# One decoder layer on one core: attention steps regrouped by head half, and the next scores moved between the halves of the transposes

## The reference

```python
scores = jnp.einsum('bhqd,bhkd->bhqk', q, k) * inv_sqrt_d
scores = jnp.maximum(scores + attention_mask, jnp.finfo(scores.dtype).min)
w = jax.nn.softmax(scores, axis=-1)
attn_output = jnp.einsum('bhqk,bhkd->bhqd', w, v)
a_scores = jnp.einsum('bhqd,bhkd->bhqk', q, a_k) * inv_sqrt_d
a_scores = jnp.tanh(gate) * jax.nn.softmax(a_scores, axis=-1)
attn_output = attn_output + jnp.einsum('bhqk,bhkd->bhqd', a_scores, a_v)
return attn_output @ Wo
```

## Time and profile before

| | us |
|---|---|
| median of 3 runs | 3539.64 (3532.39 to 3540.34) |
| the profiled execution | 3538.9 |
| its span in the trace | 3537.1 |
| TensorE busy in the span | 3087.3 |
| VectorE busy | 1727.0 |
| ScalarE busy | 1349.5 |
| mean granted TensorE clock | 0.96 |

### The profile page before, as it was taken

How to read it: one execution, slowest core, us unless ns; L and a number is a source line. 1 busy time by engine, 2 the same in 40 slices (tenths; PEclk the granted TensorE clock), 3 DMA queues, 4 the chain that set the end, 5 groups by cost and what they waited for, 6 DMA issues and landing times. The chain is left out here.

```text
span 3537.1 us, 98301 instructions
## 1 busy us (share of the span) xinstructions
PE 3087.3 (87%) x43074; PEld 1955.8 (55%) x43074; DVE 1727.0 (49%) x4747; ACT 1349.5 (38%) x3283; POOL 475.1 (13%) x591
## 2 busy tenths in 40 slices
PE   4899999999999999999984999999999999825786
PEld 3566656565655655565552666565565655512453
DVE  1545454455544454454444355555555555644613
ACT  0333333333333333333331355555555555611210
POOL 0211211112111111211110211011110111000000
PEclk9999999999999999999996999999999999967987
DMA  3010010100101001010001000000000000020311
GB/s 131 26 38 11 26 38 17 38 11 26 39 17 38 11 26 38 17 35 14 26 3 61 10 7 4 10 1 10 10 1 10 1 10 1 2 107 24 143 48 48
DMA packets 90921, 100.63 MB, mean 28 GB/s; under 512 B 38144, under 2 KB 84480, under 8 KB 89088
## 3 DMA queue, kind: packets, MB, share of 16 engines
q1 hardware_dynamic: 90496, 94.34, 8.1%
HBM read 90.00 MB, written 4.33 MB: 27 GB/s over the span
## 5 line engine op out<-in xcount | busy, mean ns | idle before, releaser
L299 PE MATMUL dr_p<-x_t,dr_w_g 128*128 128x512 f32 x1536 | 749.7, 616 | 26.8 <-DMA dr_w_g<-in_w_in 13.5
L1221 ACT ACTIVATE xa_probs<-xa_probs,xa_low 128x256 f32<-128x256 f32 x1024 | 420.9, 496 | 2.2 <-DVE xa_low L1300 2.2
L299 PEld LDWEIGHTS dr_p<-x_t,dr_w_g 128*128 128x128 f32 x1536 | 270.5, 192 | 248.4 <-issue 239.5
L1300 DVE CUSTOM_DVE_ANT_0 xa_probs<-xa_s,xa_mask 128x256 f32<-128x256 f32 x512 | 215.0, 420 | 387.8 <-PE xa_s L1134 387.8
L1146 PE MATMUL xa_t<-ident,xa_probs 128*128 128x128 f32 x2048 | 285.4, 279 | 43.7 <-ACT xa_probs_t L1228 43.7
L662 DVE SCALAR_TENSOR_TENSOR dr_acc<-dr_p,dr_taps,dr_acc 128x510 f32<-128x510 f32 (+2 forms) x384 | 285.7, 744 | 27.9 <-ACT dr_acc L556 18.9
L1228 ACT ACTIVATE xa_probs_t<-xa_t 128x512 f32<-128x512 f32 x256 | 152.8, 597 | 365.8 <-PE xa_t L1146 365.8
L1146 PEld LDWEIGHTS xa_t<-ident,xa_probs 128*128 128x128 f32 x2048 | 225.1, 142 | 109.4 <-issue 93.6
L1134 PE MATMUL xa_s<-xa_keys,xa_q_pair 32*128 32x512 f32 x1024 | 258.9, 618 | 7.7 <-DVE xa_low L1300 7.0
L696 DVE TENSOR_TENSOR dr_yx<-dr_yx,dr_g 128x512 f32<-128x512 f32 x128 | 88.1, 688 | 335.1 <-PE dr_g L363 335.1
L1310 DVE COPY xa_probs_t<-xa_t 128x512 f32<-128x512 f32 x256 | 176.3, 689 | 93.8 <-PE xa_t L1146 93.8
(11 more groups left out here) (291 smaller groups left out, 5060.6 us busy)
## 6 DMA issues: line engine op xcount, KB each, us to landing
dr_alpha<-alpha_rows SPq DMA_DIRECT2D x64, 254.0 KB, 4.2
dr_w_g<-in_w_in SPq DMA_DIRECT2D x48, 256.0 KB, 5.6
dr_alpha<-alpha_rows SPq DMA_DIRECT2D x32, 256.0 KB, 5.4
x_t<-in_x_t SPq DMA_DIRECT2D x1, 4096.0 KB, 12.1
tokens<-in_x_tok SPq DMA_DIRECT2D x1, 4096.0 KB, 21.3
dr_wo_g<-in_w_out SPq DMA_DIRECT2D x8, 512.0 KB, 3.9
xa_ctx_b<-in_ctx_t SPq DMA_DIRECT2D x8, 512.0 KB, 3.7
ff_tall<-in_fw_o SPq DMA_DIRECT2D x1, 4096.0 KB, 12.2
```

Source lines behind the costliest of these rows:

```text
L299: mm = pe.matmul(bank[:, :], w_g[:, k, m, :], x_t[:, k, 2 * S * batch:2 * S * (batch + 1)], start=(k == 0), stop=(k == KC - 1))
L1221: op = act.activation(at, at, ACT.Exp, bias=low[:, u % 3, h, j, kind:kind + 1], scale=-1.0)
L1300: op = v.tensor_tensor_reduce(out=probs[:, u % 3, h, j, kind, :], in0=bank_s[h][j][:, kind * S:(kind + 1) * S], in1=mask[:, par, q, :] if ...
```

## The change

The steps stay 128. A step v now holds one head half h of all four pairs of a tile: the four scores use the four groups of 32 partitions, where they used two of them twice. `tops`, `exps`, `scored`, `topped` and `exped` count per pair i. `weigh` runs after every step for its h, with 16 matmuls, so `probs_t` holds two steps. On PE, `score(v+1)` stands between the second and the third group of transposes of step v. Both pieces of other work stand behind the transposes: `inner` is early or else late, `outer` is late where there is an early one. On ACT `copy(u, 0)` moves ahead of the early piece. DVE's order stays.

```diff
+        def inner(u):
+            return early(u) or late(u)
+        def outer(u):
+            return late(u) if early(u) else None
...
+        def place(v):
+            g = v // 2
+            q, t = divmod(g % (QT * XT), XT)
+            return g // (QT * XT) % 2, q, t, v % 2
...
+            def turn_probs(v):
+                for i in range(4):
+                    if i == 2 and v + 1 < LAST:
+                        score(v + 1)
+                    wait(pe, exped, 4 * v + i + 1)
+                    wait(pe, copied[i % 2], 2 * v + i // 2)
...
+            def weigh(v):
+                wait(pe, copied[0], 2 * (v + 1))
+                wait(pe, copied[1], 2 * (v + 1))
...
             for u in range(LAST):
-                if u + 1 < LAST:
-                    score(u + 1)
-                if early(u):
-                    pe_make(pe, early(u))
                 turn_probs(u)
-                if late(u):
-                    pe_make(pe, late(u))
-                if u % 2:
-                    weigh(u // 2)
+                if inner(u):
+                    pe_make(pe, inner(u))
+                if outer(u):
+                    pe_make(pe, outer(u))
+                weigh(u)
...
             for u in range(LAST):
+                copy(u, 0)
                 if early(u):
                     act_take(act, early(u))
-                copy(u, 0)
                 copy(u, 1)
```

More of the change, by code:

```diff
@@ L986, in cross_phase @@
         val = a.sb("val", [P, 2, 2, KT, PAIRS, 3, XD])
[L987 to L989 removed]
+        probs = a.sb("probs", [P, 3, 4, 2, S])
+        low = a.sb("low", [P, 3, 4, 2])
+        probs_t = a.sb("probs_t", [P, 2, 4, 2, KT, P])
         mixed = a.sb("mixed", [P, 2 * 2 * P])
@@ L994, in cross_phase @@
         attn_t = a.sb("attn_t", [P, KC, P])
-        bank_s = [[a.bank(f"s{h}{j}") for j in range(2)] for h in range(2)]
+        bank_s = [a.bank(f"s{i}") for i in range(4)]
         bank_t = [a.bank(f"t{j}") for j in range(2)]
@@ L1004, in cross_phase @@
         turned_by, rotated = sem("turned_by"), sem("rotated")
-        scored = [sem(f"scored{h}") for h in range(2)]
-        topped = [sem(f"topped{h}") for h in range(2)]
-        exped = [sem(f"exped{h}") for h in range(2)]
+        scored, topped, exped = sem("scored"), sem("topped"), sem("exped")
         turned = [sem(f"turned{j}") for j in range(2)]
@@ L1125, in pe_all @@
         def pe_all(pe):
[L1126 to L1154, removed]
-                for kind in range(2):
[L1156 to L1166, removed]
+            def score(v):
+                if v % HALVES == 0:
+                    wait(pe, rotated, 4 * (v // HALVES + 1))
+                    wait_taken(pe, ("ak1", v // HALVES))
+                par, q, t, h = place(v)
+                for i in range(4):
+                    wait(pe, topped, 4 * (v - 1) + i + 1)
+                    pe.matmul(bank_s[i][:, :], q_pair[32 * i:32 * i + 32, par, t, h, q * P:(q + 1) * P],
+                              keys[32 * i:32 * i + 32, par, t].rearrange("p k n -> p (k n)"), start=True, stop=True)\
+                        .then_inc(scored, 1)
@@ new lines, in turn_probs @@
+            def turn_probs(v):
+                for i in range(4):
+                    if i == 2 and v + 1 < LAST:
+                        score(v + 1)
+                    wait(pe, exped, 4 * v + i + 1)
+                    wait(pe, copied[i % 2], 2 * v + i // 2)
+                    for kind in range(2):
+                        for kt in range(KT):
+                            at = (kind * KT + kt) * P
+                            mm = pe.transpose(bank_t[i % 2][:, at:at + P], probs[:, v % 3, i, kind, kt * P:(kt + 1) * P], ident)
+                    mm.then_inc(turned[i % 2], 1)
@@ new lines, in weigh @@
+            def weigh(v):
+                wait(pe, copied[0], 2 * (v + 1))
+                wait(pe, copied[1], 2 * (v + 1))
+                par, q, t, h = place(v)
+                if h == 0:
+                    wait(pe, mixed_taken, v // 2)
+                if v % HALVES == 0:
+                    wait_taken(pe, ("av1", v // HALVES))
+                for kind in range(2):
+                    at = (kind * 2 + h) * P
+                    for kt in range(KT):
+                        for i in range(4):
+                            mm = pe.matmul(bank_o[32 * i:32 * i + 32, at:at + P], val[:, par, kind, kt, 4 * t + i, h:h + 2],
+                                           probs_t[:, v % 2, i, kind, kt, :], start=(kt == 0), stop=(kt == KT - 1))
+                            if (kind, kt) == (1, KT - 1):
+                                mm.then_inc(weighed, 1)
@@ L1214, in act_all, with exps, copy @@
         def act_all(act):
[L1215 to L1228, removed]
+            def exps(v):
+                for i in range(4):
+                    wait(act, topped, 4 * v + i + 1)
+                    for kind in range(2):
+                        at = probs[:, v % 3, i, kind, :]
+                        op = act.activation(at, at, ACT.Exp, bias=low[:, v % 3, i, kind:kind + 1], scale=-1.0)
+                    op.then_inc(exped, 1)
+            def copy(v, m):
+                wait(act, turned[0], 2 * v + m + 1)
+                wait(act, weighed, 4 * (v - 1))
+                act.activation(probs_t[:, v % 2, 2 * m].rearrange("p k t n -> p (k t n)"), bank_t[0][:, :], ACT.Copy)\
                     .then_inc(copied[0], 1)
@@ L1246, in act_all @@
                     g = u // 2
-                    wait(act, weighed, 4 * (g + 1))
+                    wait(act, weighed, 8 * (g + 1))
                     if g:
@@ new lines, in dve_all, with tops, copy @@
+        def dve_all(dve):
+            def tops(v, m):
+                if v % HALVES == 0 and m == 0:
+                    wait(dve, mask_guarded, v // HALVES + 1)
+                wait(dve, turned[0], 2 * (v - 2))
+                wait(dve, turned[1], 2 * (v - 2))
+                par, q, t, h = place(v)
+                for i in (2 * m, 2 * m + 1):
+                    wait(dve, scored, 4 * v + i + 1)
+                    for kind in range(2):
+                        op = dve.tensor_tensor_reduce(out=probs[:, v % 3, i, kind, :], in0=bank_s[i][:, kind * S:(kind + 1) * S],
+                                                      in1=mask[:, par, q, :] if kind == 0 else zeros[:, :], scale=-1.0,
+                                                      scalar=-LOWEST_F32, op0=ALU.add, op1=ALU.min,
+                                                      accum_out=low[:, v % 3, i, kind:kind + 1])
+                    op.then_inc(topped, 1)
+            def copy(v, m):
+                wait(dve, turned[1], 2 * v + m + 1)
+                wait(dve, weighed, 4 * (v - 1))
+                dve.tensor_copy(probs_t[:, v % 2, 2 * m + 1].rearrange("p k t n -> p (k t n)"), bank_t[1][:, :]).then_inc(copied[1], 1)
@@ L1325, in dve_all @@
                 if late(u):
-                    dve_take(v, late(u))
+                    dve_take(dve, late(u))
             for use in TAIL:
-                dve_take(v, use)
+                dve_take(dve, use)
         with nc.Block() as block:
@@ L1339, in load @@
                     if b > 1:
-                        wait(sp, topped[1], 2 * DUOS * (b - 1))
+                        wait(sp, topped, 4 * HALVES * (b - 1))
                     sp.dma_start(mask[:, b % 2], mask_dram[b]).then_inc(mask_loaded, 16)
```

17 lines of the change are left out of this document (7 added, 10 removed).

## The result

The changed kernel takes 3911.54 us (median of 4 runs, 3907.63 to 3916.82), against 3539.99 for the kernel before: 1.105 times its time, 95% interval 1.103 to 1.108. The forecast was 3815 with a range of 3695 to 3895, so the direction was right, and the time lies 17 above the range.

What follows compares the result with a forecast made beforehand. TensorE's own list was taken to bound the attention. Waits added about 191 us to the profiled 3538.9, giving 3730; 77 clock falls at 1.1 us added 85, giving 3815 us, range 3695 to 3895.

Steps and rivals of the forecast that it cites:

- The scores: Four scores on TensorE run in two rounds instead of four: 1.06 us in place of 1.92.
- The two gains: On TensorE, 0.86 us a step from wider scores and 0.34 from the lost wait for ScalarE's copy; both spent again.
- The wait for VectorE's copy: Fourth group of transposes waits for a copy queued behind reductions: starts 3.5 us after the scores, about 1.95 idle every step.
- The norm's wait for the one bank: Late piece waits until VectorE has read the norm's parts: starts 5.75 us after the scores, a wait of about 1.1.
- The sum at full clock, 3730: Attention batches of 168.1 us against 144.3, about +191 us in all on the profiled 3538.9, without clock falls.
- The clock: TensorE falls to half clock in six of ten attention steps: 77 falls at 1.1 us, +85 us.
- rival 2: TensorE's clock falls in nearly every step at the high price, 141 to 218 us more: 3870 to 3950; chance 0.15.
- The heavy case: 128 clock falls on TensorE at 1.1 to 1.7 us each: 3870 to 3950 us; chance 0.15.
- The clock did not hold: Denies the rival that TensorE stays at full clock despite the waits: 3730 us, 3700 to 3755; chance 0.25.
- Slower, but by less: TensorE's waits overlap more, VectorE starting 0.3 us earlier and rope steps not waiting: 3675 us, 3600 to 3700; chance 0.07.
- Not slower: Wider scores and the lost ScalarE wait pay for everything if waits are below 1.1 us a step: 3395; chance 0.03.
- The third wait: Weighing waits for VectorE's second copy where no late piece stands between; in the sum as the 8.1 us point at d = 0.

Runs made afterwards that it cites:

- grouping only: Changed kernel with TensorE's order as in the kernel before; keeps one-head-half steps of four pairs and ScalarE's first copy ahead of its early piece: 3495.7 us.
- the filled runs: Changed kernel with unread work in TensorE's wait for VectorE's copy: two matmuls a step, 3754.4 us, or sixteen transposes a step, 3753.8 us.
- the first filled run: Changed kernel with two extra matmuls a step, results unread, ahead of the third group of transposes: 3754.4 us.
- the other pair: Changed kernel with the early piece between next scores and third group of transposes, 3630.9 us; the same with one or two extra matmuls a step, 3606.9 us.
- the two grouping-only runs: Changed kernel with the kernel before's TensorE order, 3495.7 us; the same with VectorE's second copy ahead of the last two pairs' reductions, 3470.6 us.

## Why the prediction was wrong, point by point

*The scores.* Right: two rounds, 1.08 to the next transposes (2655.93 to 2657.01), forecast 1.06. The two gains were there too: grouping only won 45 us.

*The wait for VectorE's copy.* Right: 3.52 against 3.5. The idle entry is 225.9, forecast about 250; 1.79 a step where I said 1.95, since the row of the third group is 0.66 long where I took 0.5 from start to start. The sum goes by starts and did not need it.

*The norm's wait for the one bank.* Right: the late piece at 5.68 after the scores (2725.71), forecast 5.75, waiting 1.10.

*The sum at full clock, 3730.* Borne out by the filled runs, 3754 with 41 to 51 us still at the low clock (some 15 to 19 us of time), and by the batch of 168.57 for 168.1. Steps at full clock: 11.35 for 11.4, 10.96 for 11.0, and by the score starts elsewhere in the batch 9.56 for 9.6 (d = 3), 7.52 for 7.6 (d = 5), 11.48 for 11.4 (d = 7).

*The clock.* This is the step that failed, and in its price. The term is the +85 of the sum: I took 77 falls at 1.1. The trace has 82. That the number came so near was luck: it was picked between 0 and 128 from three waits that disagreed, and nothing in the prediction says that the falls stand in the same steps of each batch. Together they cost 3907.6 (the profiled execution) less 3730, 178 us, which is also 481 us at the 0.37 below: 2.2 a fall, twice what I took and above the 1.7 that I had called the most. The 1.7 rested on a low stretch of 3.4 us, read off two places of the trace. Here 50 of the 82 last 6.8 or 10.2, and the mean is 5.9. The reason stands in the prediction itself, for rival 2 ("the stretch after it has the next wait in it"), and my sum left it out: a wait in every step is also a wait behind the fall. In each of the 50 long stretches the next wait, of the norm, the copy or the weighing, came before the last 3.4 us. That this wait is what held the clock low is read from the trace; with the first wait filled, ten of the eleven stretches left last 3.4. By the us the price was near what I took, 1.1 for 3.4 or 0.32: 162 us won for 440 us less at the low clock (the first filled run against the change, attention steps 1502.6 and 1340.5), 0.37; 24 for 62 in the other pair, 0.39; at most 0.5 is possible, for 1.2 GHz is half of 2.4. So 77 falls of 5.9 at 0.37 would have given 168, and 3898. Of the 93 us between 85 and 178, five come from the number of falls, some 13 from the price of a us, and the other 75 from the length.

*Rivals.* The heavy case (3870 to 3950, 0.15) is what came, though by longer stretches and not by more of them. The clock did not hold. "Slower, but by less" fails too: VectorE began at 1.30 and not 0.3 earlier, and the piece behind a rope turn waited 0.78. "Not slower" missed what it asked for, waits under 1.1 a step; with both waits out of the way, as it supposed, it is 3408 (I had said 3395 for a kernel without them). The waits I had called the whole cost are that: taking them out by order turned 3911 to 3408, below the 3540 of before by what the grouping gains.

*The pages.* The Trainium skill, "TensorE: Matmul & The Clock Gate", section "Why this matters for your kernels", warns only of idle gaps longer than nearly all of these. Here the trace has 82 falls, with waits of 1.79 in every step, 1.10 in 56 steps and 3.45 in only seven, and filling the first wait took 71 falls away. Its section "Part 4: PE-mode transpose" says that transposes do not count as busy in the same way; the run with sixteen transposes in the wait had 12 low stretches, that with matmuls 11, so here they count alike.

What stays open: which waits start a fall and which only prolong it. With half of the first wait filled 24 are left, with all of it 11, but no run filled the second wait alone. The third wait has a part of its own: of those 11, ten stand where the weighing waits for VectorE's second copy (d = 0 and the bare norm steps of the last batch), and in the two grouping-only runs taking that copy forward left 2 of 14. Open is also why the same waits bring a fall in one step of the batch and none in another.

## What to carry to other kernels

When work is moved later on one engine, look at what the other engines' lists have in line behind it: here VectorE's copy stood behind reductions that needed the moved scores, and TensorE needed the copy. The order on the waiting engine is part of the move, and the swap of two lines there took back 360 us of 371. Count a repeated wait on TensorE at more than its length: price the low clock by the us (0.37 of each in this kernel), and expect the low stretches to run together where the wait comes back every step.

## What the runs showed of the hardware

- Four score matmuls in four different groups of 32 partitions ran side by side: eight records in 1.14 us, where two groups took 1.99.
- With a wait of 1.79 us in every step of 7.5 to 11.5 us and 1.10 more in 56 of the 128, TensorE's clock fell to 1.2 GHz 82 times in 1503 us. 0.85 us of extra work in the first wait made it 24.
- Work that nobody reads made the kernel 157 us faster (4.0%): an idle TensorE cost more than a busy one. It is a test and no repair; the repair in order alone is at 3408.
